# Attention stage: batch 1 projected right behind batch 0, constant rows moved, and the last residual updates and statistics given new places

## The chip, the cores and the metric

The kernel runs on one core of one Trainium2 chip. The time is device microseconds of one execution. TensorE (PE) multiplies, VectorE (DVE) and ScalarE (ACT) do elementwise work and read PSUM, GpSimd (POOL) does elementwise work on SBUF alone, SyncE (SP) issues most of the DMAs. Each engine runs its own instruction list in order; semaphores tie the lists together.

## The reference, cut to what matters

Six stages are applied to x, which has 8 batches of 512 tokens of 128 numbers: a mixture of experts, a linear scan, the same mixture again, a soft mixture, attention, and the soft mixture again. The change touches the end of the fourth stage and the start of the fifth.

```python
x = x + 0.5 * _L1_ffn_ref(_layernorm(x), ...)      # soft mixture ("m")
x = x + _L1_attn_ref(_layernorm(x), w_qkv, w_out)  # attention ("a"), 16 heads of 8 numbers
# in _L1_attn_ref:
q, k, v = split(x @ w_qkv)                # per head
q = rope(q); k = rope(k)                  # x1*cos - x2*sin, x2*cos + x1*sin
scores = causal(q @ k.T * scale)
out = softmax(scores) @ v
return out @ w_out
```

## The kernel before

x stays in SBUF as 32 tiles of 128 tokens by 128 numbers, four tiles to a batch. The layer norm of the next stage needs, for each group of eight tiles, eight `bn_stats` and seven small operations on 128x8 numbers (`stats_take`, L444 to L458), a square root on ScalarE (`stats_root`, L466), and a reciprocal with one product (`stats_finish`, L475 and L476). Of the small operations L449, L450, L451, L453, L454 and L476 read two tensors of SBUF; L452 and L458 are `tensor_scalar` with one.

**End of the soft mixture.** TensorE multiplies the result of each batch into PSUM (L1332), and VectorE adds it to x (`residual(b)`, L1060, four instructions for each of the 8 batches). The order of VectorE's list there is written out by hand, with the statistics of the attention's layer norm and the first attention batch between the updates: updates 0 and 1, statistics of group 0, updates 2 and 3, `stats_take` of group 1, batch 0's rotary work, updates 4 and 5, `stats_finish` 1, group 2, updates 6 and 7, group 3.

**Attention, the front of a batch.** ScalarE normalises four tiles (L1619), TensorE transposes them (job `xt`, L1435) and multiplies them with four weights (jobs `p1`, `s1`, `p0`, `s0`, L1438; 1 is K, 0 is Q, and `s` has the weights turned by half a head). ScalarE copies a `p` result to `raw` (L1639), VectorE multiplies an `s` result with the sine (L1575) into `swapped`. `rotate` (six operations, L1781 to L1794) makes of both the rotated matrix and cuts it into three bf16 parts in `cut`. It runs on VectorE for Q of batch 0 and on GpSimd for all others. Except operation 0, whose second input is the cosine, each reads what the one before wrote and waits for it; all have two inputs in SBUF. `stack_part` then copies the parts with DMAs from SP into the stacks of the batch (L1809), 12 DMAs of 64 KB for Q and 12 for K. There are four stacks of each; two groups of rows of a K stack hold the constant minus one, written by GpSimd memsets (L1707), first those of stack 0, and after K of batch 0 those of stacks 1 to 3.

**Attention, the body.** Body i runs over 16 heads. For each head TensorE makes the scores of batch i (L1470) in three PSUM banks, and VectorE takes row maxima (`row_maxima`, L1565, four instructions with their accumulator reads). Twelve heads later TensorE makes the scores again, transposed and with the maximum subtracted (L1483), ScalarE takes exponentials (L1627), GpSimd masks (`causal`, L1722 and L1725), and TensorE sums with the values (L1498). The maxima reach the stack by a chain of their own: `cut_maxima` on GpSimd (L1738 to L1741) when eight heads are done, a transpose (job `m0`, L1446, at head 9), a copy (L1647), and two DMAs from SP (`maximum`, L1818). Jobs stand at fixed heads: in body 0 batch 1's `p0`, `s0`, `p1`, `s1` at heads 0 to 3, the values (`v`, L1441) at 7, batch 2's five front jobs at 10 to 14. TensorE enters body 0 when all of x is updated (`x_done`) and the stacks of batch 0 are there.

**Order on GpSimd in the attention before:** constants of stack 0, K of batch 0, constants of stacks 1 to 3, the buffers of the values (L1712, L1714), K and Q of batch 1 (`for m in range(2)`: Q first), then `cut_maxima(0, 0)`, the first half of Q of batch 2, `causal(0, 0)`, the other half, `cut_maxima(0, 1)`, `causal(0, 1)`. **Order on SP before:** stacks of batch 0, of batch 1 (Q, then K), then `maximum(0, 0)`, Q of batch 2, and so on.

## Time and profile before

| | |
|---|---|
| median of 3 runs | 1003.56 us (1002.2 to 1004.35) |
| the profiled execution | 1003.07 us, span 1001.3 us |
| TensorE, busy | 777.1 us |
| VectorE, busy | 658.6 us |
| ScalarE, busy | 507.3 us |
| GpSimd, busy | 442.9 us |
| granted TensorE clock, mean | 0.875 of 2.4 GHz |

The span is first to last instruction; the time of the execution is 1.8 us longer. No engine is busy throughout, so the end is set by chains that go from engine to engine. The attention stage lies from about 505 us to 885 us.

### The profile page before, as it was taken

How to read it: one execution, taken by the hardware profiler on the slowest of the kernel's cores; microseconds unless marked ns; L12 is line 12 of the kernel's file. 1: busy time of each engine (PE TensorE's matmuls, PEld its weight loads, DVE VectorE, ACT ScalarE, POOL GpSimd, SP SyncE). 2: the span in 40 equal slices, each digit the busy share in tenths (PEclk: the TensorE clock that was granted, in tenths of full speed). 3: DMA queues.
4: the chain of work that ended last, by engine and by line, in shares of the span. 5: the costliest groups of instructions: out<-in, count | busy, mean ns of one | idle time of the engine just before them, and what ended most of it. 6: DMA issues, size and time to landing. Idle time of an engine off the chain costs nothing.

```text
span 1001.3 us, 18706 instructions
## 1 busy us (share of the span) xinstructions
PE 777.1 (78%) x5564; PEld 512.1 (51%) x5564; DVE 658.6 (66%) x2367; ACT 507.3 (51%) x1371; POOL 442.9 (44%) x563
## 2 busy tenths in 40 slices
PE   4788983798498960499666979988999899729977
PEld 3678872547288860377651323333333333327757
DVE  4565654775865548856387776877777886566634
ACT  5333331606133323866411466767767677687650
POOL 1047773400277762411156577486585633261100
PEclk9999997895599995699895678999989999959999
DMA  6731113002011113000021342242231200000002
GB/s 154 230 92 49 50 47 99 1 1 84 13 46 52 50 37 82 0 1 1 1 45 32 59 58 37 31 63 34 38 54 31 48 4 3 1 1 1 1 1 84
DMA packets 53426, 42.95 MB, mean 43 GB/s; under 512 B 9861, under 2 KB 48722, under 8 KB 53328
## 3 DMA queue, kind: packets, MB, share of 16 engines
q1 hardware_dynamic: 46784, 31.74, 15.4%
q0 software_dynamic: 4992, 9.32, 3.4%
q8 instruction: 47, 0.77, 0.3%
q10 hardware_dynamic: 1552, 0.70, 0.3%
q14 instruction: 51, 0.42, 0.2%
HBM read 18.27 MB, written 11.40 MB: 30 GB/s over the span
## 4 chain that ended last, share of the span: by engine, by line
PE 42%; DVE 18%; POOL 12%; issue 12%; ACT 9%; DMA 5%; ACTq 1%; DVEq 1%; POOLq 0%; SPq 0%
PE psum L1498 5%; POOL arena L832 4%; DMA result_rows<-arena,scatter_row 3%; PE psum L1269 3%; PE psum L747 3%; DVE half_stats L444 3%; PE psum L1483 2%; DVE cst L1565 2%; PE psum L1232 2%; PE psum L1241 2%; PE psum L1438 2%; PE psum L787 2%; DVE x L694 2%; PE psum L1332 2%; PE psum L799 2%
## 5 line engine op out<-in xcount | busy, mean ns | idle before, releaser
L1565 DVE CUSTOM_DVE_ANT_0 cst<-psum,rot 128x512 bf16<-128x512 f32 (+3 forms) x512 | 219.1, 487 | 64.4 <-PE psum L1470 54.8
L1627 ACT ACTIVATE arena<-psum 128x512 f32<-128x512 f32 (+1 forms) x384 | 178.3, 530 | 51.5 <-PE psum L1483 46.0
L832 POOL DMA_INDIRECT arena<-xhat_rows,gather_row x78 | 76.6, 982 | 148.3 <-DVE gather_row L634 125.2
L1470 PE MATMUL psum<-arena 48*128 48x512 bf16 (+3 forms) x512 | 121.8, 330 | 14.5 <-DVE row_max L1565 10.6
L1483 PE MATMUL psum<-arena 51*128 51x512 bf16 (+3 forms) x512 | 114.9, 315 | 8.8 <-ACT arena L1627 7.1
L1722 POOL TENSOR_SCALAR_AFFINE_SELECT arena<-arena 128x384 f32<-128x384 f32 x128 | 63.6, 521 | 96.4 <-ACT arena L1627 96.4
L1498 PE MATMUL psum<-arena 128*32 128x512 f32 (+3 forms) x1024 | 98.3, 482 | 7.5 <-POOL arena L1725 7.5
L841 POOL DMA_INDIRECT result_rows<-arena,scatter_row x78 | 79.1, 1014 | 30.2 <-issue 22.2
L787 PE MATMUL psum<-arena 128*128 128x128 f32 x624 | 87.5, 286 | 4.2 <-DVE arena L649 4.2
L799 PE MATMUL psum<-arena 128*128 x624 | 89.5, 287 | 0.3
L715 ACT ACTIVATE arena<-psum,gate_b1T 128x128 f32<-128x128 f32 x156 | 48.7, 363 | 68.1 <-PE psum L787 68.1
L787 PEld LDWEIGHTS psum<-arena 128*128 128x128 f32 x624 | 79.8, 200 | 5.8 <-DVE arena L649 5.7
L799 PEld LDWEIGHTS psum<-arena 128*128 128x128 f32 x624 | 76.7, 194 | 7.5 <-issue 5.0
L1483 PEld LDWEIGHTS psum<-arena 51*128 51x128 bf16 x512 | 38.7, 96 | 75.2 <-ACT arena L1627 46.2
L1470 PEld LDWEIGHTS psum<-arena 48*128 48x128 bf16 x512 | 38.9, 98 | 60.5 <-DVE row_max L1565 50.0
L655 DVE TENSOR_SCALAR arena<-psum,gate_b1T 128x128 f32<-128x128 f32 x156 | 47.7, 347 | 24.1 <-issue 18.2
L466 ACT ACTIVATE st<-st 128x8 f32<-128x8 f32 x24 | 4.9, 209 | 115.0 <-DVE st L458 114.8
L649 DVE COPY arena<-arena 128x512 f32 x78 | 41.0, 525 | 32.8 <-issue 25.6
L709 ACT COPY arena<-psum 128x128 f32<-128x128 f32 x78 | 20.7, 265 | 68.7 <-PE psum L778 68.7
L1225 PE MATMUL psum<-cst,xh 128*128 128x128 f32 x64 | 10.6, 293 | 53.3 <-POOL xh L1109 53.3
L1109 POOL TENSOR_TENSOR xh<-arena,st 128x512 f32<-128x512 f32 x16 | 18.8, 1182 | 68.1 <-PE psum L1225 66.3
L444 DVE BATCH_NORM_STATS2 half_stats<-x 128x6 f32<-128x128 f32 x192 | 39.4, 278 | 7.0 <-DMA x<-in_L_attn_x 6.2
(247 smaller groups left out, 1649.1 us busy)
## 6 DMA issues: line engine op xcount, KB each, us to landing
arena<-cut SPq DMA_DIRECT2D x192, 64.0 KB
xhat_rows<-xh SPq DMA_DIRECT2D x16, 256.0 KB, 2.3
arena<-result_rows SPq DMA_DIRECT2D x8, 512.0 KB, 6.0
x<-in_L_attn_x SPq DMA_DIRECT2D x4, 512.0 KB, 7.4
arena<-in_L_ffn_w SPq DMA_DIRECT2D x1, 2048.0 KB, 9.6
out<-x SPq DMA_DIRECT2D x4, 512.0 KB, 3.2
arena<-xhat_rows,gather_row POOLq DMA_INDIRECT x78, 2.5
result_rows<-arena,scatter_row POOLq DMA_INDIRECT x78, 2.3
```

The source lines that it names most:

```text
L444: nc.vector.bn_stats(half_stats[:, t, :], x[:, t, :]).then_inc(stat_sem, 1)
L715: last = nc.scalar.activation(hidT[:, k % 2, c, :], bank[4 + k % 2][:, c * P:c * P + P], ACT.Relu, bias=b1T[:, bass.ds(e * FC + c, 1)])
L787: last = pe.matmul(bank[(2 if c < FC // 2 else 4) + k % 2][:, c * P:c * P + P], w1_tile[:, k % 2, c * P:c * P + P], xgT[:, k % 2, :], star ...
L799: last = pe.matmul(bank[6 + k % 2][:, 0:D], hidT[:, k % 2, c, :], w2[:, bass.ds(e, 1), c, :], start=False, stop=(c == FC - 1))
L832: pool.indirect_dma_start(xg[:, j % AHEAD, :], None, xhat_dram, bass.IndirectOffsetOnAxis(gather_row[:, j:j + 1], 0)).then_inc(gathered[j ...
L841: pool.indirect_dma_start(yrow_dram, bass.IndirectOffsetOnAxis(scatter_row[:, j:j + 1], 0), yg[:, j % 3, :], None, bounds_check=T * P - 1, ...
L1470: mm = pe.matmul(to[:, col:col + (k + 1) * P], q_stack[b % STACKS][rows, h, k * P:k * P + P], k_stack[b % STACKS][rows, h, 0:(k + 1) * P], ...
L1483: mm = pe.matmul(bank[MAX_BANKS + number % EXP_BANKS][:, col:col + S - k * P], k_stack[b % STACKS][rows, h, k * P:k * P + P], q_stack[b % ...
L1498: last = pe.matmul(bank[6][32 * j:32 * j + 32, k * P:], v_aug[b % 2][:, k, HALF * a + h, :], prob_e[g % 2][:, j, E_AT[k]:E_AT[k] + S - k * ...
L1565: last = nc.vector.tensor_tensor_reduce(masked_scores[:, number % 2, col:col + n_keys], frm[:, col:col + n_keys], mask[:, S - n_keys:], 1. ...
L1627: nc.scalar.activation(prob_e[g % 2][:, j, first:last], bank[MAX_BANKS + number % EXP_BANKS][:, 0:last - first], ACT.Exp, scale=DH ** -0.5 ...
L1722: pool.affine_select(blocks, blocks, pattern=[[0, 3], [1, P]], compare_op=ALU.is_ge, fill=0.0, base=0, channel_multiplier=-1)
```

## The change

- Batch 1's five front jobs leave the bodies 0. TensorE runs them as a second list (`SECOND`) right behind the last product of the soft mixture, ScalarE right behind batch 0's; they have PSUM banks, a `swapped` and a `cut` buffer of their own (`swapped_second`, `cut_second`).
- VectorE's list: updates 4 and 5, `s1` of batch 1, update 6, `s0` of batch 1, `stats_finish` 1, `stats_take` 2, update 7, `stats_finish` 2, group 3.
- GpSimd: the buffers of the values are filled before the attention's first wait; the constants of stacks 0 and 1 stand ahead of K of batch 0, then K and Q of batch 1, then the constants of stacks 2 and 3.
- SP: stacks of batch 0, K of batch 1, `maximum(0, 0)`, then Q of batch 1. Batch 0's copies count on a semaphore of their own (`stack_first`), and rotations from batch 2 on wait, at operation 1, for the stack copies of the batch before, as they did.
- ScalarE's normalisation of batch 2 waits for two statistics groups instead of four, that of batch 4 for all four.

```diff
@@ stats and residuals of the mixture, VectorE
                     stats_take(dve, n + 1, 1)
-                    first_batch[n + 1]["vector"](dve)
+                    first_batch[n + 1]["vector"](dve, 0)
                     residual(4)
                     residual(5)
+                    first_batch[n + 1]["vector"](dve, 1)
+                    residual(6)
+                    first_batch[n + 1]["vector"](dve, 2)
                     stats_finish(dve, n + 1, 1)
                     stats_take(dve, n + 1, 2)
+                    residual(7)
                     stats_finish(dve, n + 1, 2)
-                    residual(6)
-                    residual(7)
                     stats_take(dve, n + 1, 3)
                     stats_finish(dve, n + 1, 3)
@@ TensorE, behind the last product
+                if n + 1 in first_batch:
+                    first_batch[n + 1]["tensor"](pe, 1)
@@ jobs
-                steps_in = ("xt", "p1", "s1", "p0", "s0") if b == 0 else ("xt", "p0", "s0", "p1", "s1")
+                steps_in = ("xt", "p1", "s1", "p0", "s0") if b < 2 else ("xt", "p0", "s0", "p1", "s1")
                 if b < 2:
-                    at_body, at_slot = ((-1,) * 5, (0, 1, 2, 3, 4)) if b == 0 else ((-1, 0, 0, 0, 0), (5, 0, 1, 2, 3))
+                    at_body, at_slot = (-1,) * 5, tuple(range(5 * b, 5 * b + 5))
@@ TensorE, entry of the bodies
-                job(*jobs_at(-1, 5)[0])
                 pe.wait_ge(x_done[n], T)
+                pe.wait_ge(s["misc_read"], 10)
                 for i in BODIES[1:]:
                     if maxing(i):
-                        for m in range(2):
-                            pe.wait_ge(stack_in[m], STACK_DMAS * (i + 1))
+                        for m in range(2 if i else 0):
+                            pe.wait_ge(stack_in[m], STACK_DMAS * i)
+                        if i == 0:
+                            pe.wait_ge(stack_first, 2 * STACK_DMAS)
@@ ScalarE
                 stats_root(act, n, 1)
+                normalise(1)
+                for step, b, m in SECOND:
+                    job(step, b, m)
                 stats_root(act, n, 2)
-                normalise(1)
                 stats_root(act, n, 3)
-                job(*jobs_at(-1, 5)[0])
@@ GpSimd
+                for i in range(2):
+                    setup(pool.memset(v_aug[i][:], 0.0))
+                    for e in range(2):
+                        setup(pool.memset(v_halves[i][:, :, e, :, 16 * e + DH:16 * e + DH + 1], 1.0))
...
+                constant_rows(0)
+                constant_rows(1)
...
-                for m in range(2):
-                    rotate(pool, pool, 1, m, 0, 6)
+                rotate(pool, pool, 0, 1, 0, 6)
+                rotate(pool, pool, 1, 1, 0, 6)
+                rotate(pool, pool, 1, 0, 0, 6)
+                pool.wait_ge(turned_in[0], 12)
+                constant_rows(2)
+                constant_rows(3)
@@ rotate, operation 1
-                        if b:
-                            engine.wait_ge(stack_in[m], STACK_DMAS * b)
+                        if b >= 2:
+                            engine.wait_ge(stack_in[m], STACK_DMAS * (b - 1))
@@ SP
                 for part in range(3):
                     for m in (1, 0):
                         stack_part(sp, 0, m, part)
-                for m in range(2):
-                    for part in range(3):
-                        stack_part(sp, 1, m, part)
+                for part in range(3):
+                    stack_part(sp, 1, 1, part)
+                maximum(0, 0)
+                for part in range(3):
+                    stack_part(sp, 1, 0, part)
                 for i in BODIES[1:]:
...
-                    if 0 <= i < B:
+                    if 1 <= i < B:
                         maximum(i, 0)
```

## Rows read from the trace of the kernel before

**Rows 1.** The page: the span, and busy time of each engine.
```profile
span 1001.3 us, 18706 instructions
PE 777.1 (78%) x5564; PEld 512.1 (51%) x5564; DVE 658.6 (66%) x2367; ACT 507.3 (51%) x1371; POOL 442.9 (44%) x563
```
**Rows 2.** The chain of waits, 565 to 583 us: start, length, what.
```profile
568.85 2.61 issue
571.46 1.28 POOL cut L1786
...
581.01 0.37 POOL arena L1725
...
581.43 1.92 PE psum L1498 x5
```
**Rows 3.** The timeline of VectorE, 507 to 538 us: start, length, instructions.
```profile
507.78 1.65 DVE L444 BATCH_NORM_STATS2 half_stats<-x 128x6 f32<-128x128 f32 x8
...
510.31 0.17 DVE L458 TENSOR_SCALAR st<-st 128x8 f32<-128x8 f32 x1
...
518.53 1.52 DVE L1792 TENSOR_TENSOR raw<-raw,cut 128x512 f32<-128x512 f32 x1
...
520.69 2.15 DVE L1060 SCALAR_TENSOR_TENSOR x<-psum,inv_c,x 128x128 f32<-128x128 f32 x8
...
525.11 4.96 DVE L452 TENSOR_SCALAR st<-st 128x8 f32<-128x8 f32 x1
...
530.31 1.62 DVE L458 TENSOR_SCALAR st<-st 128x8 f32<-128x8 f32 x1
...
538.00 0.68 DVE L1565 CUSTOM_DVE_ANT_0 cst<-psum,rot 128x512 bf16<-128x512 f32 x1
```
**Rows 4.** The timeline of TensorE, same columns.
```profile
511.10 1.02 PE L1438 MATMUL psum<-xT,wqk_turned 128*128 128x512 f32 x2
511.96 5.52 PE L1332 MATMUL psum<-arena 128*128 128x128 f32 x48
...
538.17 2.08 PE L1438 MATMUL psum<-xT,wqk 128*128 128x512 f32 x2 [2.40 <-ACT xT L1633]
```
**Rows 5.** The timeline of VectorE in body 0; brackets: idle before, and releaser.
```profile
553.99 0.69 DVE L1565 CUSTOM_DVE_ANT_0 cst<-psum,rot 128x512 bf16<-128x512 f32 x1
...
555.63 0.69 DVE L1565 CUSTOM_DVE_ANT_0 cst<-psum,rot 128x512 bf16<-128x512 f32 x1
...
558.82 0.69 DVE L1565 CUSTOM_DVE_ANT_0 cst<-psum,rot 128x512 bf16<-128x512 f32 x1 [1.47 <-PE psum L1470]
...
570.64 0.69 DVE L1575 TENSOR_TENSOR arena<-psum,rot 128x512 f32<-128x512 f32 x1
```
**Rows 6.** The timeline of GpSimd, 490 to 559 us.
```profile
490.43 3.65 POOL L1707 MEMSET arena<- 32x2048 f32 x2 [34.72 <-PE psum L1312]
...
519.56 10.48 POOL L1707 MEMSET arena<- 32x6144 f32 x2
...
550.62 1.26 POOL L1781 TENSOR_TENSOR raw<-raw,rot 128x512 f32<-128x512 f32 x1
...
557.11 1.15 POOL L1794 TENSOR_TENSOR cut<-raw,cut 128x512 bf16<-128x512 f32 x1
```
**Rows 7.** The timeline of SP's DMA issues.
```profile
513.06 15.77 SPq L1809 DMA_DIRECT2D arena<-cut  x24
...
562.25 1.57 SPq L1818 DMA_DIRECT2D arena<-arena  x2
```
**Rows 8.** One window: us, granted clock, DMA share, GB/s.
```profile
531.00:532.00 1.00, 0.50 0.04 6
```
**Rows 9.** The timeline of VectorE at 882 us, statistics beside GpSimd products.
```profile
882.72 0.16 DVE L450 TENSOR_TENSOR st<-half_stats 128x8 f32<-128x8 f32 x1
882.80 1.23 DVE L451 TENSOR_TENSOR st<-half_stats 128x8 f32<-128x8 f32 x1
```
**Rows 10.** The timeline of GpSimd there.
```profile
879.05 4.96 POOL L1101 TENSOR_TENSOR arena<-arena,gamma 128x512 f32<-128x512 f32 x4 [10.73 <-ACT arena L1125]
```

More of the change, by code:

```diff
@@ L250, in build @@
         swapped_first = carve(arena3, 8192, (2, S))
+        swapped_second = carve(arena3, 9216, (2, S))
+        cut_second = carve(arena3, 6144, (2, 3, S), BF16)
         cut = sb("cut", [P, 2, 3, S], BF16)
@@ L1416, in swapped_of, with cut_of, tensor @@
             def swapped_of(b):
-                return swapped if b else swapped_first
+                return (swapped_first, swapped_second, swapped)[min(b, 2)]
+            def cut_of(b):
+                return cut_second if b == 1 else cut
             FIRST = [found for hh in range(5) for found in jobs_at(-1, hh)]
-            def tensor(pe, only_first=False):
+            SECOND = [found for hh in range(5, 10) for found in jobs_at(-1, hh)]
+            def tensor(pe, ahead=None):
                 def job(step, b, m):
@@ L1427, in job @@
                         pe.wait_ge(s["misc_read"], 1)
+                    elif 6 <= m < 10:
+                        pe.wait_ge(s["misc_read"], 6)
                     elif m == ORDER["n1", B - 1]:
@@ L1510, in side @@
                             job(step, b, m)
-                if only_first:
+                if ahead is not None:
                     pe.wait_ge(att_w, 1)
-                    for step, b, m in FIRST:
+                    for step, b, m in (FIRST, SECOND)[ahead]:
                         job(step, b, m)
                     return
-                job(*jobs_at(-1, 5)[0])
                 pe.wait_ge(x_done[n], T)
+                pe.wait_ge(s["misc_read"], 10)
                 for i in BODIES[1:]:
                     if maxing(i):
-                        for m in range(2):
-                            pe.wait_ge(stack_in[m], STACK_DMAS * (i + 1))
+                        for m in range(2 if i else 0):
+                            pe.wait_ge(stack_in[m], STACK_DMAS * i)
+                        if i == 0:
+                            pe.wait_ge(stack_first, 2 * STACK_DMAS)
                     for hh in range(H):
@@ L1546, in tensor, with vector @@
                         side(i, hh, 2)
-            def vector(dve, only_first=False):
+            def vector(dve, ahead=None):
                 steps = Chain(dve, s["steps"])
@@ L1593, in job @@
                         dve.sem_inc(s["misc_read"], 1)
-                if only_first:
+                if ahead == 0:
                     for step, b, m in FIRST:
@@ L1598, in vector @@
                     rotate(dve, nc.vector, 0, 0, 0, 6)
+                    return
+                if ahead:
+                    job(*SECOND[2 * ahead])
                     return
@@ L1693, in scalar, with stack_set_up @@
                             job(step, b, m)
-            SET_UP = 10
+            VALUES_SET_UP = 6
+            def stack_set_up(b):
+                return VALUES_SET_UP + 2 * (b + 1)
             def gpsimd(pool):
+                setup = Chain(pool, s["set_up"])
+                for i in range(2):
+                    setup(pool.memset(v_aug[i][:], 0.0))
+                    for e in range(2):
+                        setup(pool.memset(v_halves[i][:, :, e, :, 16 * e + DH:16 * e + DH + 1], 1.0))
                 if n and stages[n - 1] == "m":
@@ L1703, in gpsimd, with constant_rows @@
                 pool.wait_ge(zeroed, 2)
-                setup = Chain(pool, s["set_up"])
-                for first, many in ((0, 1), (1, STACKS - 1)):
+                def constant_rows(b):
                     for rows in (slice(32, 64), slice(96, 128)):
-                        setup(pool.memset(arena2[rows, 2048 * first:2048 * (first + many)], MINUS_ONES))
-                    if first == 0:
-                        rotate(pool, pool, 0, 1, 0, 6)
-                        pool.wait_ge(turned_in[1], 6)
-                for i in range(2):
-                    setup(pool.memset(v_aug[i][:], 0.0))
-                    for e in range(2):
-                        setup(pool.memset(v_halves[i][:, :, e, :, 16 * e + DH:16 * e + DH + 1], 1.0))
+                        setup(pool.memset(arena2[rows, 2048 * b:2048 * (b + 1)], MINUS_ONES))
+                constant_rows(0)
+                constant_rows(1)
                 def causal(b, pair):
@@ L1772, in rotate @@
             def rotate(engine, issue, b, m, first, last):
-                part = [cut[:, m, r, :] for r in range(3)]
+                part = [cut_of(b)[:, m, r, :] for r in range(3)]
                 v, w = raw[:, m, :], swapped_of(b)[:, m, :]
@@ L1800, in stack_part @@
                 engine.wait_ge(turned_in[m], 6 * b + PART_READY[part])
-                if b == 1:
-                    engine.wait_ge(s["set_up"], 4)
+                if b < STACKS:
+                    engine.wait_ge(s["set_up"], stack_set_up(b))
                 if part == 0 and b >= STACKS:
@@ L1809, in stack_part @@
                             engine.dma_start(to[b % STACKS][64 * a + DH * r:64 * a + DH * r + DH, :, :],
-                                             cut[64 * a:64 * a + 64, m, part, :]).then_inc(stack_in[m], 16)
+                                             cut_of(b)[64 * a:64 * a + 64, m, part, :]).then_inc(stack_in[m] if b else stack_first, 16)
             def sync(sp):
-                sp.wait_ge(s["set_up"], 2)
                 def maximum(b, half):
```

17 lines of the change are left out of this document (9 added, 8 removed).

## The prediction, on record before the changed kernel ran

> **What bounds the kernel now.** I read the page first: no engine is busy for the whole span [rows 1], so some chain of waits sets the end. Next the chain of waits around the change. Its last link ahead of the steady part of the attention is GpSimd: operation 1 of the rotation of Q of batch 2 starts at 571.46, and TensorE's first sums (L1498) start at 581.43, right behind a mask on GpSimd [rows 2]. That is 9.97 us of GpSimd work in one queue. The reader is to see that TensorE, VectorE and ScalarE all stand behind these sums. So I ask one question of each edit: when does that operation 1 start afterwards? What follows the sums is unchanged work and moves with them.
>
> In the trace operation 1 waits for the sine product of batch 2, which VectorE makes at 570.64 (+0.69) [rows 5]. Going back from there: body 0 on VectorE starts at 538.00 [rows 3], its head 8 at 558.82 [rows 5]. The start is late because VectorE's statistics stand behind GpSimd's memsets, 4.96 and 1.62 us for instructions of 0.17 [rows 3, 6]. The body is slow because batch 1's projections sit in it, 2.08 us each at the half clock [rows 4, 8].
>
> **The change part by part.** All times are against the profiled execution, 1003.07 us with a span of 1001.3; the median of the runs is 0.5 us above it.
>
> *Value buffers and constants on GpSimd.* The first go into 34.7 us of idle time before 490.43, the constants of stacks 0 and 1 take 2 x 3.65 = 7.3 us from there, to 497.7, and K of batch 0 is not due until 510 [rows 6]. VectorE reads PSUM then. Cost nothing; if the cover went, 3.65 us more ahead of K.
>
> *Batch 1's front on TensorE.* The products of the mixture end at 511.96 + 5.52 = 517.5 [rows 4]. A transpose group and its copy take about 1.2 us by batch 0's pattern, then four projections at 0.86 us each, the distance of 511.10 and 511.96 [rows 4]: K's raw at about 520.4, the last sine input at 522.5. TensorE was idle there, so this costs nothing.
>
> *Body 0 without those jobs.* Heads of VectorE are 555.63 - 553.99 = 1.64 us apart where nothing holds it [rows 5]. Eight heads are 13.16, and the values job still holds it for 1.47: 14.63 us against 558.82 - 538.00 = 20.82 [rows 3, 5]. Gain 6.2 us.
>
> *VectorE up to body 0.* Batch 0's rotation ends at about 520.8. Then: four updates 4 x 1.07 = 4.3 (eight instructions took 2.15 [rows 3]); two sine products 1.4; two groups of statistics, each 1.65 + 1.05 (507.78 to 510.48, GpSimd idle [rows 3]), 5.4; finishes and the root 1.4. Sum 13.3, to about 533.2, if nothing stands in the way. The stacks of batch 0 have landed by 531.2 (24 issues end at 528.83, and the DMA share is 0.04 from 531 on [rows 7, 8]), so they would not hold it.
>
> But GpSimd now rotates K and Q of batch 1 over just this stretch: K's second operation can start at 523.6, behind the sine product, and eleven operations, at 557.11 + 1.15 - 550.62 = 7.64 us per six [rows 6], take it to about 538. The rotation on VectorE shows what that does: an operation with two SBUF inputs takes 1.52 us and ends behind GpSimd's, though its own work is some 0.69 [rows 3, 5]. The small instructions show it too: beside GpSimd products of 1.24 us, L450 got through in 0.16 and L451, issued 0.08 later, took 1.23 [rows 9, 10]. So the two engines take turns, and a chain of dependent small instructions pays one GpSimd operation for each turn. One `stats_take` has five turns (L449 with L450; L451; L452 with L453; L454; L458), the finish one (L476).
> - finish 1: about 0.8.
> - group 2: the first turn half an operation, 0.7, four more at 1.3: 5.5 to 5.9. It ends at about 534.7; update 7 then ends at 535.8.
> - finish 2: 0.3 to 1.3. Group 3: one turn behind the last rotation, 0.8, then L452 and L458 behind the constants of stacks 2 and 3, 1.82 us each memset [rows 6]: 1.5 each. The existing trace has just these two instructions held by memsets [rows 3].
>
> Sum 9.6 to 11, taken as 10.1: body 0 starts at 543.3, which is 5.3 us later than before. Bounds: 533.2 if it never has to wait, 546 if every turn pays in full.
>
> By the Trainium skill, page "SBUF — State Buffer", section "Who interferes with whom", an instruction of VectorE with two SBUF inputs is kept out by a GpSimd instruction that reads SBUF, not by one that only writes, and one in a 2-port mode by either; the holder keeps the ports for its whole instruction. From the memset rows alone one would charge L452 and L458 only and reach 536.9; with the rule, 543.3. The rotation rows and the rows at 882 us agree with the rule.
>
> *Head 8 afterwards:* 543.3 + 14.63 = 557.9, a gain g = 6.2 - 5.3 = 0.9 us. The sine product of batch 2, eight heads' jobs unchanged, is ready at 571.33 - 0.9 = 570.4.
>
> *SP's queue.* `maximum(0, 0)` was issued until 562.25 + 1.57 = 563.82 [rows 7]; its SP wait ends with the copy behind head 9, so now at 562.9. Q of batch 1 stands behind it in SP's queue although its parts are ready at 538. Twelve issues at 15.77 / 24 = 0.66 us are 7.9 us, and the last lands some 2.4 us after its issue (528.83 to 531.2 [rows 7, 8]): 573.2. Operation 1 of Q of batch 2 waits for that, and behind it on GpSimd stand `causal(0, 0)`, `cut_maxima(0, 1)` and `causal(0, 1)`, for which TensorE's sums wait. So it starts at 573.2 instead of 571.46: the gate is later by 1.7 us. In general the shift is 2.6 - g, or d - 3.6 with d the lateness of body 0. The sums move to 583.1. TensorE's own entry of body 1 needs the same copies, but falls after 573 anyway. A transfer faster by 1 us gives back 1 us.
>
> *Waits of ScalarE for statistics, other buffers:* all of it is ready 20 us before it is used; nothing.
>
> Sum: +1.7 us. 1003.07 + 1.7 = 1004.8 for such an execution, 1003.56 + 1.7 = 1005.3 for the median.
>
> **The rivals.**
> - *The ports matter little (faster).* Only `tensor_scalar` waits, as under the memsets [rows 3], so body 0 starts at 536.9, d = -1.1: shift -4.7, 998.9 us. With no wait at all it is d = -4.8 and -8.4, 995.2. For it: L450 slipped through behind L449 [rows 9]. Against it: L451 did not, nor did the rotation [rows 3].
> - *Partial turns.* Three instructions pass in a turn, or GpSimd comes out of step: d = 2.5, shift -1.1, 1002.5 us.
> - *The rotation runs into group 3 (slower).* VectorE's turns also delay GpSimd, and if the rotation still runs at 540, group 3 has its five turns behind rotations and then a memset besides: 3.2 us more, d = 8.5, shift +4.9, 1008.5 us. It decides from d = 5.6 on, where the loss passes 2 us.
> - *The Q copies hold nobody*, because they land before the sine product: shift -g = -0.9, 1002.7 us. Against it: 10.3 us from issue to landing stand against the 7.5 between the end of `maximum` and operation 1 [rows 2, 7].
>
> **How the numbers follow.** A difference under 0.2% (2.0 us) can't be told from none here. My forecast has 0.55, with its own range of d from 4 to 6.5, 1004.0 to 1006.5, and is on the slow side of 1005.6 in somewhat under half of it. The ports mattering little has 0.16, partial turns 0.12, the longer rotation 0.12, copies that hold nobody 0.05. Faster: 0.16 and a few hundredths, 0.18. Slower: 0.12 + 0.27 = 0.39. Same: the rest, 0.43. The range goes from 998.5, just under the first rival, to 1008.0; outside are its extreme form and half of the longer rotation, about 0.13, and what the half clock after a longer wait of TensorE may add.
>
> **What the profile will show.** L449 to L458 of groups 2 and 3 at over 1 us in several instructions, and L1565 first at 542 to 545. Head 8 behind it by 14.6 us. SP's twelve Q copies issued right behind L1818, at about 563. GpSimd's L1786 of batch 2 idle before it, released by a DMA and not by VectorE. L1498 first at about 583, and from there the old distances. I am wrong if L1565 starts before 538, or if L1786 follows the sine product at once.

## The result, and the profile after

The changed kernel takes 1008.79 us (median of 20 runs, 1004.06 to 1013.34) against 1003.85 us of the kernel before (20 runs, 1001.76 to 1010.47). The ratio is 1.0043, 95% interval 1.0025 to 1.0061: slower by about 4 us. The median lies outside the predicted range, which ended at 1008.0. The profiled execution took 1006.37 us, 3.3 more than that of before.

The page, engine totals. They differ from before [rows 1] by 6 us of busy TensorE and hardly elsewhere; the extra time is waiting.

```profile
span 1004.6 us, 18726 instructions
PE 771.1 (77%) x5564; PEld 510.9 (51%) x5564; DVE 659.7 (66%) x2367; ACT 507.7 (51%) x1371; POOL 443.6 (44%) x567
```

The chain of waits after, ahead of the first sums of the attention: start, length, what. In the kernel before, the same operation 1 began at 571.46 behind a sine product, the sums at 581.43 [rows 2].

```profile
567.74 6.38 DMA arena<-arena
...
574.28 1.28 POOL cut L1815
...
583.82 0.37 POOL arena L1750
...
584.23 1.92 PE psum L1512 x5
```

The gate is 2.8 us later, and a DMA stands where VectorE stood. Now VectorE's timeline from the end of batch 0's rotation to the first head of body 0, which answers to [rows 3].

```profile
526.28 0.52 DVE L478 SCALAR_TENSOR_TENSOR st<-st 128x8 f32<-128x8 f32 x1
526.72 1.63 DVE L446 BATCH_NORM_STATS2 half_stats<-x 128x6 f32<-128x128 f32 x8
528.38 0.88 DVE L451 TENSOR_TENSOR st<-half_stats 128x8 f32<-128x8 f32 x1
529.18 0.16 DVE L452 TENSOR_TENSOR st<-half_stats 128x8 f32<-128x8 f32 x1
...
529.46 1.03 DVE L454 TENSOR_SCALAR st<-st 128x8 f32<-128x8 f32 x1
530.40 0.15 DVE L455 SCALAR_TENSOR_TENSOR st<-st 128x8 f32<-128x8 f32 x1
530.59 1.12 DVE L456 TENSOR_TENSOR st<-st 128x8 f32<-128x8 f32 x1
531.74 0.17 DVE L460 TENSOR_SCALAR st<-st 128x8 f32<-128x8 f32 x1
...
538.13 1.83 DVE L460 TENSOR_SCALAR st<-st 128x8 f32<-128x8 f32 x1
...
540.55 0.68 DVE L1581 CUSTOM_DVE_ANT_0 cst<-psum,rot 128x512 bf16<-128x512 f32 x1
...
555.26 0.69 DVE L1581 CUSTOM_DVE_ANT_0 cst<-psum,rot 128x512 bf16<-128x512 f32 x1 [1.46 <-PE psum L1484]
...
567.02 0.69 DVE L1591 TENSOR_TENSOR arena<-psum,rot 128x512 f32<-128x512 f32 x1
```

GpSimd after: four products of batch 1's rotation (the last is at 536.92), the memsets, and the product that waits.

```profile
529.31 1.15 POOL L1823 TENSOR_TENSOR arena<-raw,arena 128x512 bf16<-128x512 f32 x1
530.42 1.26 POOL L1810 TENSOR_TENSOR raw<-raw,rot 128x512 f32<-128x512 f32 x1
531.76 1.27 POOL L1815 TENSOR_TENSOR arena<-raw,arena 128x512 bf16<-128x512 f32 x1
...
536.92 1.15 POOL L1823 TENSOR_TENSOR arena<-raw,arena 128x512 bf16<-128x512 f32 x1
538.13 7.36 POOL L1736 MEMSET arena<- 32x2048 f32 x4
...
574.28 1.27 POOL L1815 TENSOR_TENSOR cut<-raw,arena 128x512 bf16<-128x512 f32 x1 [9.02 <-DMA arena<-arena]
```

SP's issues after, against [rows 7].

```profile
529.71 7.89 SPq L1838 DMA_DIRECT2D arena<-arena  x12
558.68 1.56 SPq L1845 DMA_DIRECT2D arena<-arena  x2
560.35 7.99 SPq L1838 DMA_DIRECT2D arena<-arena  x12
```

What the reader is to see: the small instructions of the statistics pay about 1 us three times in each chain of seven (L451, L454, L456), each time for one GpSimd product. They end as that product ends (L456 at 530.59 + 1.12 = 531.71, the product at 530.42 + 1.26 = 531.68). What starts before GpSimd's next product passes, as L460 does: it starts at 531.74, that product at 531.76. Body 0 starts at 540.55 instead of 538.00, and its head 8 at 555.26 instead of 558.82 [rows 5]. So VectorE is ahead again by 3.6 us, and the sine product of batch 2 is ready at 567.71. GpSimd doesn't use it: it waits until 574.28 for the stack copies of Q of batch 1, issued from 560.35 on. The gain was made and then not collected.

A second thing is in the times. Of all 28 runs of the changed kernel (the 20, and the 8 of the first experiment) 13 lie at 1004.1 to 1007.1 (median 1005.8) and 15 at 1010.5 to 1013.3 (median 1011.4), with nothing between. The profiled execution is of the lower group. The median over all therefore says less than the two groups do.

### The profile page after: what moved, and what is told of

Its sections match the earlier page's. It is cut to its first block, busy times and chain, and to the rows that moved or that the text cites. A ratio compares the mean times of both kernels' runs of the same rounds, so it can differ in the third digit from the quotient of the medians.

```text
span 1004.6 us, 18726 instructions
## 1 busy us (share of the span) xinstructions
PE 771.1 (77%) x5564; PEld 510.9 (51%) x5564; DVE 659.7 (66%) x2367; ACT 507.7 (51%) x1371; POOL 443.6 (44%) x567
## 4 chain that ended last, share of the span: by engine, by line
PE 38%; DVE 19%; issue 13%; POOL 13%; ACT 9%; DMA 4%; DVEq 1%; ACTq 1%; SPq 1%; POOLq 0%
PE psum L1512 5%; POOL arena L834 4%; PE psum L1273 3%; PE psum L1236 3%; PE psum L749 3%; PE psum L1245 3%; DVE cst L1581 3%; DVE half_stats L446 3%; PE psum L1497 2%; DVE x L696 2%; POOL result_rows L843 2%; DMA result_rows<-arena,scatter_row 2%; PE psum L1336 2%; PE psum L745 2%; ACT arena L1646 1%
## 5 line engine op out<-in xcount | busy, mean ns | idle before, releaser
L1512 PE MATMUL psum<-arena 128*32 128x512 f32 (+3 forms) x1024 | 98.3, 482 | 13.3 <-POOL arena L1750 13.3
L1512 PEld LDWEIGHTS psum<-arena 128*32 128x32 f32 x1024 | 24.2, 111 | 39.4 <-issue 15.8
```

Of the source, the lines that this page charges most:

```text
L1512: last = pe.matmul(bank[6][32 * j:32 * j + 32, k * P:], v_aug[b % 2][:, k, HALF * a + h, :], prob_e[g % 2][:, j, E_AT[k]:E_AT[k] + S - k * ...
```

## The experiments

Each kernel is timed beside the kernel before on the same chip. "The gate" is the start of operation 1 of the rotation of Q of batch 2 on GpSimd (after: 574.28, the first sums 584.23). The profiled executions start the attention up to 5 us apart (VectorE's first rotary product at 511.9 to 517.2), so where it matters I compare distances inside one profile.

### after_again: the changed kernel once more

> The changed kernel once more, beside the variants below. Theory A (the Q copies of batch 1, issued behind the copies of the maxima, hold GpSimd's operation 1 of batch 2 and through it the first sums): the gate at about 574 and the sums at 584 us again, TensorE idle some 7 us ahead of them, the time about 4 us over the kernel before. Theory B (what is lost is lost to the granted clock, which lies in other places in each execution): gate and sums may be the same, but the times spread over 8 us and fall in two groups, as the 20 runs did (1004 to 1007 and 1010 to 1013).

Measured: 1010.62 us (1004.47 to 1011.98, 8 runs), ratio 1.0051 (1.0029 to 1.0074). Profile: body 0 at 538.85, head 8 at 553.56, gate at 572.43 behind an idle of 8.86 ended by a DMA, sums at 582.38, everything 1.7 to 1.9 us earlier than in the first profile, with nearly the same distances. The result repeats, and so do the two groups (3 and 5 of 8).

### q_first: Q's copies of batch 1 ahead of the maximum

```
                 for part in range(3):
                     stack_part(sp, 1, 1, part)
-                maximum(0, 0)
                 for part in range(3):
                     stack_part(sp, 1, 0, part)
+                maximum(0, 0)
```

> SP issues the Q copies of batch 1 ahead of the copies of the maxima, nothing else changes. Theory A: the Q copies land long before body 0 is done, operation 1 of batch 2 follows the sine product, at 567.7 instead of 574.3 us, the sums come 6.5 us earlier, at about 577.8, and the time falls by 6 to 7 us against the changed kernel, to some 2 to 3 us under the kernel before. Theory B: the order of the copies is not what costs; the time falls by less than 2 us.

Measured: 1002.21 us (999.69 to 1006.97, 12 runs), ratio 0.9988 (0.9965 to 1.001). Operation 1 in its profile, the sums, and SP's issue of the maxima:

```profile
569.36 1.27 POOL L1815 TENSOR_TENSOR cut<-raw,arena 128x512 bf16<-128x512 f32 x1 [2.58 <-issue]
```
```profile
579.33 1.93 PE L1512 MATMUL psum<-arena 128*32 128x512 f32 x8 [1.47 <-POOL arena L1750]
```
```profile
560.21 1.56 SPq L1845 DMA_DIRECT2D arena<-arena  x2
```

GpSimd now follows the sine product (568.54 + 0.69) at once. With a body 0 that began 1.5 us later than in the changed kernel, the sums come 4.9 us earlier. The order in SP's queue was the loss at the gate: undoing that one part takes the changed kernel from slower to level with before. Five of the 12 times are again in a higher group (1004.7 to 1007.0), above seven at 999.7 to 1002.4.

### parts_swapped: another order of Q's copies

```
-Q_PART, K_PART = (0, 0, 1, 0, 2, 1), (0, 1, 0, 2, 0, 1)
+Q_PART, K_PART = (0, 1, 0, 2, 0, 1), (0, 0, 1, 0, 2, 1)
```

> The changed kernel with the part lists of Q and K exchanged, so that the Q copies now write the row blocks (0, 2, 4), (1, 5), (3) one after another and K the blocks (0, 1, 3), (2, 5), (4). Nothing else. The Q copies of batch 1 took 13.8 us from the first issue to landing, K's some 10. Theory C (the order of the row blocks a copy writes sets its speed): Q's twelve now land about 10.3 us after their first issue, operation 1 of batch 2 at about 571, sums at 581, 3 us less than the changed kernel. Rival (they are slow because body 0 computes beside them, or because they are Q's): 13.5 us again and the same time.

Measured: 1008.11 us (1004.09 to 1013.37, 12 runs), ratio 1.0043 (1.0024 to 1.0061). From Q's first issue at 561.38 to the gate at 574.97 are 13.6 us, as in the changed kernel (13.9). The pattern of row blocks is not what makes the copies slow. Its profiled execution, 1012.51 us with a span of 1010.8, happened to be one of the higher group. The windows of the attention's tail show it: us, busy time of PE, PEld, DVE, ACT and POOL, granted clock, DMA share, GB/s; first the changed kernel, then parts_swapped.

```profile
842.00:852.00 10.00, 8.44 (x73) 2.78 (x73) 5.45 (x28) 7.11 (x16) 5.01 (x14) 0.91 0.01 2
852.00:862.00 10.00, 9.95 (x85) 3.88 (x85) 1.56 (x4) 7.41 (x17) 2.70 (x6) 0.92 0.01 3
862.00:872.00 10.00, 7.83 (x77) 3.22 (x73) 6.50 (x30) 9.16 (x19) 4.10 (x9) 1.00 0.01 2
```
```profile
842.00:852.00 10.00, 8.35 (x75) 2.84 (x75) 6.38 (x32) 8.05 (x19) 5.18 (x15) 1.00 0.00 1
852.00:862.00 10.00, 10.00 (x60) 3.77 (x59) 1.56 (x4) 5.77 (x13) 2.11 (x5) 0.50 0.02 5
862.00:872.00 10.00, 9.90 (x64) 3.79 (x60) 0.95 (x3) 5.77 (x14) 2.70 (x6) 0.64 0.00 0
```

The changed kernel's TensorE is at 1.2 GHz for 3.4 us here; that of parts_swapped for 17 us (852.1 to 869.2), with TensorE busy nearly all of it. The same sums (L1512) begin at 850.10 and, three groups on, at 871.76 in the changed kernel, at 851.03 and 877.68 in parts_swapped: it falls back from 0.9 to 5.9 us, 5 us, about the distance of the two groups. Just ahead of it TensorE had two gaps. The changed kernel, which stays at 1.2 GHz for 3.4 us only, has the same two; parts_swapped first, then the changed kernel:

```profile
849.37 1.05 PE L1497 MATMUL psum<-arena 51*128 51x512 bf16 x4 [0.70 <-ACT arena L1646]
851.03 1.07 PE L1512 MATMUL psum<-arena 128*32 128x512 f32 x8 [0.61 <-POOL arena L1750]
```
```profile
848.44 1.05 PE L1497 MATMUL psum<-arena 51*128 51x512 bf16 x4 [0.70 <-ACT arena L1646]
850.10 1.92 PE L1512 MATMUL psum<-arena 128*32 128x512 f32 x8 [0.62 <-POOL arena L1750]
```

So the gaps stand ahead of the fall of the clock in both; they don't tell whether it lasts 3.4 or 17 us.

### constants_early: all memsets ahead of the attention, and q_first

```
-                constant_rows(0)
-                constant_rows(1)
+                for b in range(STACKS):
+                    constant_rows(b)
...
-                pool.wait_ge(turned_in[0], 12)
-                constant_rows(2)
-                constant_rows(3)
```

and the edit of q_first.

> On top of q_first, GpSimd writes the constants of all four stacks in one row ahead of K of batch 0 (7.3 us more, into idle time before 510). Theory A with the port waits: the last statistics instruction, held 1.83 us by a memset, is free; body 0 starts 1.8 us earlier and so do the gate and the sums; 1.5 to 2 us less than q_first. Theory B (clock places decide): no difference to q_first beyond the spread.

Measured: 999.99 us (997.83 to 1006.51, 12 runs, 4 of them in a higher group), ratio 0.9966 (0.9942 to 0.999). The chain of group 3 pays its three turns (0.80, 1.03, 1.12) as in the changed kernel, but L460 behind them passes in 0.17 instead of 1.83:

```profile
538.02 1.12 DVE L456 TENSOR_TENSOR st<-st 128x8 f32<-128x8 f32 x1
539.18 0.17 DVE L460 TENSOR_SCALAR st<-st 128x8 f32<-128x8 f32 x1
```

A little is given back earlier: the long memset (491.81, 14.78 us for eight) now meets group 0's L460, which takes 1.61 at 505.01. The profile is one of the higher group: TensorE at 1.2 GHz from 842.3 to 862.8.

### rotation_after_stats: batch 1's rotation held until the statistics are done

constants_early, and ahead of `rotate(1, 1)` on GpSimd:

```
+                pool.wait_ge(ready_sem, GROUPS * n + GROUPS)
```

> On top of constants_early, GpSimd starts to rotate K and Q of batch 1 only when all statistics are finished, so no instruction of VectorE's statistics meets a GpSimd product. Port theory: the statistics of groups 2 and 3 take 2.7 us each instead of 5.2 and 7.0; body 0 starts when finish 3 is done, 6 to 7 us earlier than in q_first (relative to the mixture's last product), and the time falls by 4 to 6 us against q_first, unless the rotation of batch 1, now 15 us later, delays cut_maxima(0, 0), which stands behind it: it would end at about 550 with head 8 at 549, so by at most 1 to 2 us. Rival (the statistics are slow of themselves, or TensorE's start of body 0 is what decides): less than 2 us.

Measured: 996.08 us (993.92 to 1005.09, 12 runs), ratio 0.9941 (0.9914 to 0.9969). Group 3 of the statistics and the first head, with no GpSimd product beside it:

```profile
534.70 0.17 DVE L451 TENSOR_TENSOR st<-half_stats 128x8 f32<-128x8 f32 x1
...
535.07 0.17 DVE L454 TENSOR_SCALAR st<-st 128x8 f32<-128x8 f32 x1
...
535.35 0.17 DVE L456 TENSOR_TENSOR st<-st 128x8 f32<-128x8 f32 x1
535.55 0.17 DVE L460 TENSOR_SCALAR st<-st 128x8 f32<-128x8 f32 x1
...
536.32 0.69 DVE L1581 CUSTOM_DVE_ANT_0 cst<-psum,rot 128x512 bf16<-128x512 f32 x1
```

From the first update after the rotation (524.00) to body 0 are 12.3 us; in the changed kernel 540.55 - 521.28 = 19.3. The 7.0 us between them are six turns beyond an instruction's own 0.17, (0.88 + 1.03 + 1.12 + 0.80 + 1.03 + 1.12) - 6 x 0.17 = 5.0, the memset's 1.83 - 0.17 = 1.7, and L478's 0.52 - 0.17. Nothing else moved. This is the cost of the GpSimd work placed beside the statistics, shown by taking it away.

### filled_q_first and filled: two products in TensorE's gaps

In TensorE's loop of the last bodies (q_first, and the changed kernel alone):

```
+                        if i == B and hh < 2:
+                            pe.wait_ge(s["max_read"], 3 * H * B)
+                            pe.matmul(bank[hh][:], ident, rot[:, R_COS:R_COS + S], start=True, stop=True)
```

The two products write PSUM banks that are free by then; nobody reads them. They stand in the first two heads of the last body but one, where the gaps are.

> q_first with two more products of 512 columns (0.86 us each at 2.4 GHz, results not used) in the first two heads of the body behind the last row maxima, where TensorE has two gaps of 0.6 to 0.7 us; the output is unchanged. Theory B (the upper group of times, 5 to 6 us over the lower, are executions in which the clock falls just behind these gaps and stays at 1.2 GHz through the tail of the attention): the upper group gets rarer or goes, the lower stays within 1 us. Rival (the groups have another cause, or two products are too little): 4 or 5 of 12 executions stay in the upper group.

> The changed kernel with the same two products. Theory B: the share of the upper group (15 of 28 executions of the changed kernel) falls clearly, the median falls from 1009 to 1006, and what is left of the loss against the kernel before, 2 to 3 us, is theory A's. Rival: half of the executions stay at 1010 to 1013.

Measured: filled_q_first 999.68 us (998.6 to 1001.83, 12 runs), ratio 0.9955 (0.9936 to 0.9974); filled 1004.95 us (1003.62 to 1009.14, 12 runs), ratio 1.0012 (0.9996 to 1.0028). The lower groups hardly moved (q_first 999.7 to 1002.4, after 1004.1 to 1007.1); the groups 5 to 6 us above them are gone but for one run of filled, at 1009.14. The attention of filled_q_first runs 2.1 us ahead of that of q_first (first sums at 577.26 and 579.33), where the two gaps end at 844.09 and 845.75. So the products stand where the gaps were, in TensorE's timeline of filled_q_first:

```profile
841.17 1.13 PE L1543 MATMUL psum<-rot,cst 128*128 128x512 f32 x2 [0.59 <-DVE row_max L1584]
...
842.87 1.13 PE L1543 MATMUL psum<-rot,cst 128*128 128x512 f32 x2
```

and both profiles have full clock from 842 to 862 us, here filled_q_first:

```profile
842.00:852.00 10.00, 9.77 (x78) 3.94 (x78) 1.56 (x4) 8.19 (x18) 4.26 (x10) 1.00 0.02 5
852.00:862.00 10.00, 9.74 (x87) 3.78 (x83) 3.47 (x16) 8.26 (x20) 4.08 (x9) 1.00 0.01 2
```

By the single times, then, about 2 of the changed kernel's 4.9 us at the median lie in its lower group (1005.8 against 1003.85 of before), and about 3 in how often it falls into the higher one: 15 of 28 runs, where the kernel before does so (over 1009 us) in 3 of the 20 runs beside it and in 8 of the 90 beside the experiments. f2_filled_before below tests this split, and it doesn't come out whole.

### f1_best: all together

rotation_after_stats with the two filling products.

> The kernel with batch 1's rotation held behind the statistics of batch 0, with the two filling products of the filled kernels added to TensorE's stream. Theory (the higher group of times is TensorE left at its lower clock in attention's tail, and the two products remove that): one group of times only, that of the lower group before, 993.9 to 996 us, a ratio of 0.990 to 0.991 of the kernel before, with full clock at 842 to 862 us of the profile. Rival (the groups come from elsewhere and were absent in the filled kernels by luck): again 3 to 5 of 12 times some 5 to 10 us above the others, ratio 0.994.

Measured: 996.13 us (992.41 to 997.96, 6 runs), ratio 0.9912 (0.9892 to 0.9931). No time lies in a higher group, and 842 to 862 us are at full clock. The median equals that of rotation_after_stats (996.08), whose kernel before was 1.4 us faster on its chip; by ratio f1_best is ahead of it, 0.9912 against 0.9941. The spread, 5.6 us, is wider than the 2 us expected, and six runs are few to say that a group is gone. It is the best kernel of the study, about 9 us ahead of before.

### f2_filled_before: the two products in the kernel before

> The kernel before with the two filling products alone. Theory: the few times of the kernel before at 1009 to 1010.5 us are gone, and the median moves by less than 1 us, so that the fill by itself is worth next to nothing to the kernel before and several us to the one after. Rival (the products help in every stage): 2 us or more faster at the median.

Measured: 1002.2 us (1000.98 to 1003.32, 12 runs), ratio 0.9974 (0.9959 to 0.9988). The high times are gone and the spread is 2.3 us. But the median moved by 2.2 us, not by under 1: the kernel with the fill is that much faster, and its TensorE, at half clock at 847.0 to 850.4 before, now is not. Its profile shows only 0.7 us of this behind the first sums, where the products stand (from there to the end of the span 419.2 us instead of 419.9); where the rest comes from is not shown. So my theory held on the groups, and its claim that the fill gives before next to nothing did not.

With the products in both kernels the change still costs 1.0012 against 0.9974 of before, 0.4% or 3.8 us; from the two intervals I estimate 1.6 to 6.0, and the two were timed on different chips. So the loss doesn't fall to the 2 us of the lower groups once the higher one is taken away. That 3 of the 4.9 us are the higher group's is a reading of the single times, and this comparison doesn't bear it out. Against a filled kernel before, f1_best is 1002.2 - 996.13 = 6.1 us ahead; that is what all the edits but the fill are worth.

### f3_own_wait: GpSimd waits for what it needs

```
-                        if b >= 2:
-                            engine.wait_ge(stack_in[m], STACK_DMAS * (b - 1))
+                        if b == 2:
+                            engine.wait_ge(stack_first, 2 * STACK_DMAS)
+                        elif b > 2:
+                            engine.wait_ge(stack_in[m], STACK_DMAS * (b - 2))
```

and batch 1's copies count on a semaphore of their own, for which TensorE waits at its entry of body 1 and SP's order is kept as changed.

> The changed kernel, where the copies of batch 1 count on a semaphore of their own: GpSimd's first product of the next body waits for those of batch 0 alone, as the values need, and TensorE waits for those of batch 1 at its entry of body 1. Theory A (GpSimd's queue holds the body's start, since its product waits for a copy it has no use for): op1 at about 568 us in place of 574.3, the first sums at about 578 in place of 584.2, and the time within 1.5 us of the kernel with Q's copies first (1002.2). Rival (TensorE's own entry, which waits for the same copies or for their rows, decides): the first sums at 580 or later, less than half of the gain of Q's copies first, 1005.5 us or more.

Measured: 1011.13 us (1006.05 to 1011.98, 7 runs, 6 of them over 1010), ratio 1.0071 (1.0057 to 1.0085), slower than the changed kernel. Its gate:

```profile
569.97 1.27 POOL L1821 TENSOR_TENSOR cut<-raw,arena 128x512 bf16<-128x512 f32 x1 [2.57 <-issue]
```

and TensorE, at its entry of body 1, at the first sums, in the body, and at the sums of the next group of heads:

```profile
576.34 0.37 PE L1498 MATMUL psum<-arena 51*128 51x512 bf16 x1 [2.31 <-DMA arena<-arena]
...
579.93 1.94 PE L1513 MATMUL psum<-arena 128*32 128x512 f32 x8 [0.88 <-POOL arena L1754]
...
588.33 0.39 PE L1498 MATMUL psum<-arena 51*128 51x512 bf16 x1 [2.46 <-DMA arena<-arena]
...
590.90 1.94 PE L1513 MATMUL psum<-arena 128*32 128x512 f32 x8
```

At the gate theory A is right: operation 1 follows the sine product (569.15 + 0.69), with a body 0 that began 2.1 us later than in the changed kernel, and the sums come 4.3 us earlier. But the second sums are 10.97 us behind the first, in q_first 8.58 (579.33 to 587.91). The 2.46 us are the copies of the row maxima, issued at 582.91. Ahead of them in the DMA queue are 24 stack copies, issued from 562.48 on and moving at about 68 GB/s, 0.95 us each from the fourth on: they need until about 585. In q_first the first 12 of these 24 had landed by 549. The median of 1011 is not the price of these copies: six of the seven times are in the higher group. The profiled one, 1006.05, is in the lower, and its span of 1004.3 us is level with the changed kernel's 1004.6, so that nearly all of the 4.3 us gained at the first sums is lost again behind them, 2.4 of it (10.97 - 8.58) by the second sums. So both theories missed: the semaphore hid a transfer that was late anyway, and letting GpSimd pass brought the lateness to the next user. Rather than loosen the wait, the copies had to go earlier.

### f4_copies_late: where do slow copies come from?

```
+                sp.wait_ge(turned_in[0], 12)
+                sp.wait_ge(turned_in[1], 12)
                 for part in range(3):
                     stack_part(sp, 1, 1, part)
                 for part in range(3):
                     stack_part(sp, 1, 0, part)
```

in rotation_after_stats.

> The kernel with batch 1's rotation held behind the statistics, where SP issues the 24 copies of batch 1 only once both rotations of batch 1 have ended, about 553 us. Theory D (the first dozen copies after a pause of the queues go at 62 to 68 GB/s, those right behind them at 98 to 104): slow for about 12 us from 553, then fast, whatever the engines do. Rival (GpSimd's products or ScalarE's exponentials beside the copies slow them): from 553 on about 100 GB/s until the exponentials of the next body begin at about 560, then 62 to 75. The time itself tells nothing of this (about 1005 us, since the body waits for copies that are issued later).

Measured: 1015.68 us (one run), 10 us more than I had expected, with the first sums at 592.58. Both theories fall in one window, that of f4_copies_late from 562 to 574 us (columns as above):

```profile
562.00:574.00 12.00, 0.00 (x0) 0.00 (x0) 0.00 (x0) 0.00 (x0) 0.00 (x0) 0.50 0.57 66
```

No engine works at all, and the copies still move at 66 GB/s. From the fourth on each of the 24 takes 0.98 us, those of the second dozen too. So it is not the engines beside them, and not only the first dozen behind a pause. And in the kernel rotation_after_stats, whose engines do the same work in this stretch, the second half of the same 24 copies, issued 12 us earlier, ran at 116 GB/s:

```profile
552.00:557.00 5.00, 4.92 (x21) 1.99 (x20) 4.59 (x23) 2.12 (x5) 0.69 (x3) 0.50 0.56 116
```
```profile
552.00:557.00 5.00, 5.00 (x20) 2.38 (x20) 4.59 (x21) 1.55 (x4) 0.25 (x1) 0.50 0.47 74
```

(the first line is rotation_after_stats, the second f4_copies_late, which starts its copies at 552.4).

### half_by_half and late_mixed: the copies' order among themselves

half_by_half is the changed kernel with the two loops in `stack_part` exchanged; late_mixed is f4_copies_late with K and Q in turns:

```
-                for r in range(len(parts)):
-                    if parts[r] == part:
-                        for a in range(2):
+                for a in range(2):
+                    for r in range(len(parts)):
+                        if parts[r] == part:
...
-                for part in range(3):
-                    stack_part(sp, 1, 1, part)
-                for part in range(3):
-                    stack_part(sp, 1, 0, part)
+                for part in range(3):
+                    for m in (1, 0):
+                        stack_part(sp, 1, m, part)
```

> The changed kernel, where a stack's copies go out half by half: all copies of the first 64 source rows of a part before those of the last 64, in place of alternately. The same 64 KB copies, the same number, the same waits. Theory N (copies that overlap get in each other's way when they touch the same rows, so the order decides the pace): the twelve copies of Q of batch 1 take another time than the 0.98 us each that they took, either more (1.2 or above) or near the 0.66 at which SP issues them; at 0.66 the first sums come 3 us earlier and the time is about 1003 for the lower group. Rival (the pace does not hang on which copies are neighbours): 0.98 us each from the fourth on, operation 1 at about 574, the time as that of the changed kernel.

> The kernel with the copies of batch 1 issued late, with its 24 copies in the order of batch 0's: K and Q in turns, part by part. Nothing else runs from 562 on, as in the run before. Theory N (neighbouring copies decide the pace): the 24 go at the 0.66 to 0.70 us each of batch 0's 24, so that they have landed by about 569 instead of 576. Rival (the order of K and Q has no part in it): 0.98 us each throughout, as before.

Measured: half_by_half 1006.03 us (1003.84 to 1012.64, 10 runs), ratio 1.0022 (0.9991 to 1.0053), gate at 573.68 behind an idle of 9.12 ended by a DMA, the Q copies 0.98 us each from the fourth on. late_mixed 1013.43 us (one run), 0.94 us each from the third on, 69 or 70 GB/s with all engines idle. The order is not it either. The median of half_by_half is lower than that of the changed kernel only because 3 of its 10 times, not 15 of 28, are in the higher group; its seven others, 1003.8 to 1006.8, are where the changed kernel's lower group is.

The trace of the kernel before had the slow pace already. Its copies of batch 1 start behind a pause of SP, and the window 549 to 557 us lies within them (columns as above, DMA share and GB/s last):

```profile
549.00:557.00 8.00, 6.90 (x21) 2.25 (x21) 7.00 (x32) 0.00 (x0) 7.61 (x7) 0.50 0.58 72
```

In all fifteen profiles, by the times at which the packets ended, the stack copies starting up to 575 us that are fast from their first on are batch 0's and those that SP issues right behind them, as the 24 in q_first from 531.39 on (99 GB/s from 533 to 547 us). Copies behind a later pause are slow from the third or fourth on, for about a dozen (rotation_after_stats) or to the end (f4_copies_late). Why is open.

## Why the prediction was wrong

It is wrong by size, 1005.3 against 1008.79. The mechanism at the gate is right. The direction is right by luck: with body 0 later by the measured 2.55 us, the prediction's own formula (d - 3.6) puts the gate 1.1 us earlier than before and the time at 1002.5 us, and it was the copies, 3.6 us slower than forecast, that made the gate late. Two terms of the sum were mis-sized and nearly cancelled (VectorE's turns and the duration of the Q copies), and one that the sum put at nothing, what lies behind the first sums, is where the median left the forecast. Step by step:

- **The value buffers, batch 1's front on TensorE, the eight heads at 14.63 us.** The heads took 555.26 - 540.55 = 14.71. Right.
- **VectorE takes turns with GpSimd, body 0 later by 5.3 us.** Measured 540.55 - 538.00 = 2.55, of which 0.57 was there at the start already (the rotation ended at 521.35, not 520.8). The mechanism is right and shown by rotation_after_stats; the term was mis-sized, 10.1 us of waits where 7.0 were measured. (The work without waits was right: its parts add up to 12.5 us, not to the 13.3 written, and 520.8 + 12.5 is the 533.3 that the text goes on with; measured 12.3.) I charged each chain five turns at 1.3. It pays three, of 0.80 to 1.12: L452 and L453 follow L451, and L455 follows L454, in 0.15 or 0.16 each, because they start before GpSimd's next product does, and so does L460, the last, which passes in 0.17 (the predicted case "partial turns", with a chance of 0.12, had d = 2.5). Only one L460 met a memset, not two. By the Trainium skill, page "SBUF — State Buffer", section "Who interferes with whom", an instruction with two SBUF inputs is kept out by a GpSimd instruction that reads SBUF. The trace agrees for L451 and L456 (0.88 and 1.12). L454, a `tensor_scalar` with one SBUF input, pays as well (1.03). That L452 and L453 pass right behind L451, and the last `tensor_scalar` L460 in 0.17, the rule alone would not have told me.
- **Head 8 ahead by 0.9 us.** Measured 3.56: follows from the step above.
- **Q's twelve copies hold the gate, 10.3 us from issue to landing.** That they hold it is right, and shown by q_first. Their duration is the step at the gate that failed: 574.28 - 560.35 = 13.9 us, at 0.98 us each from the fourth on instead of 0.66, 3.6 us more. I had taken the pace of batch 0's 24 copies, which SP's issue sets, for that of any dozen, though the trace before has 72 GB/s for batch 1's.
- **The gate later by 1.7 us.** Measured 2.8, or 2.25 without the 0.57. Two errors nearly cancelled: SP came free 3.6 us earlier than in the kernel before instead of 0.9 us, a gain of 2.7 over the forecast, and the copies took 3.6 us more. That the lower group, 1005.8, lies near the sum's 1005.3 is by this luck.
- **"From there the old distances."** This is the step that failed for the time: what follows the sums was called "unchanged work" that moves with them, a term of nothing. In the lower group it holds: from the first sums to the end of the span are 420.4 us, before 419.9. In the higher group it doesn't. No profile of the changed kernel itself is of that group; the two that are, of parts_swapped and constants_early, have 425.9 and 427.1 us there, and TensorE at 1.2 GHz for 17.1 and 20.5 us in the tail instead of 3.4. The prediction left room for "the half clock after a longer wait of TensorE" and no more, and a rival for it was missing. With the two products in, one of 42 times is in a higher group (filled_q_first, filled, f1_best, f2_filled_before), which bears out that the clock in the tail makes the group. Why this kernel falls into it more often than the one before stays open: the kernel before has the same two gaps, 0.70 and 0.62 us, up to 845.05 and 846.72. And how much of the 4.9 us the group accounts for isn't settled either (see f2_filled_before).

Of the rivals, "the Q copies hold nobody" was wrong, the longer rotation and the ports mattering little as well. Where the change's gain went: body 0 is 6.1 us shorter, 2.6 go to the turns and the memset ahead of it, and the 3.6 left stand unused behind SP's queue until q_first lets them through. All of it collected and protected gives the 996 us of f1_best.

What stays open is the pace of the copies. The same 64 KB copies go at 0.66 us (98 GB/s, SP's pace), at 0.53 to 0.6 (116 GB/s in rotation_after_stats), and at 0.98 (66). Excluded by runs as the whole cause: the engines' work beside them, the pattern of row blocks, halves in turns or one after the other, K and Q in turns. A pause of SP ahead of them goes with the slow pace in every profile except for batch 0's copies, and in q_first, without the pause, the same twelve Q copies of batch 1 are fast; but they also go 20 us earlier there, and batch 0's are fast behind a longer pause, so this isn't shown to be the cause. That the slow pace holds with every engine idle agrees with the Trainium skill, page "SBUF — State Buffer", section "Who interferes with whom", by which DMA reaches SBUF through ports that no engine shares. The same page, section "Door 1: The DMA port swizzle", says that a transfer's rate depends on how many of 16 ports its partitions reach; a copy here reads 64 rows and writes 8 in fast and slow bursts alike, and no run changed these numbers.

## What to carry to other kernels

When a producer is made earlier, follow its data through every in-order queue to the consumer; here the gain stood behind one later instruction in SP's queue, and moving twelve DMAs ahead of two gave it back. Don't place GpSimd products beside a chain of tiny dependent VectorE instructions: the chain of seven took 3.5 us here (528.38 to 531.91) instead of 1.0. And look at single times before a median: if they fall in two groups, compare the granted clock in a profile of each before explaining the difference by the change.

## What the runs showed of the hardware

- Beside GpSimd products of 1.15 to 1.27 us, the chain L451 to L460 pays three waits of 0.80 to 1.12 us. Which three is the same in both groups of the statistics; those that start before GpSimd's next product pass in 0.15 to 0.17. Beside a memset the last one takes 1.83.
- Twelve or 24 SBUF to SBUF copies of 64 KB, in 1 KB packets, go at 66 GB/s in some bursts (f4_copies_late) and at 98 to 116 in others. The DMA engines' share is 0.57 at 66 GB/s and 0.56 at 116, so what differs there is the time of a packet. All engines idle changes nothing (66 GB/s).
- TensorE at 1.2 GHz for 17 us in the tail (parts_swapped), although busy nearly all of that time, and for 3.4 us in the changed kernel, behind the same gaps of 0.70 and 0.61 or 0.62 us. With two products of 512 columns (1.13 us each) in these gaps the granted clock is full from 842 to 862 us, and one time of 42 is left in the group 5 to 6 us above the others.
